# Query projection in four wide products instead of six, with the halves added on the vector engine

## The reference

```python
x = layer_norm(image_embeds, ln1_g, ln1_b)
l = layer_norm(latents, ln2_g, ln2_b)
q = l @ Wq
kv = jnp.concatenate([x, l], axis=1) @ Wkv
k, v = jnp.split(kv, 2, axis=-1)
w = jax.nn.softmax(einsum('bhqd,bhkd->bhqk', q * scale, k * scale))
out = einsum('bhqk,bhkd->bhqd', w, v)        # then out @ Wo, the residual, the experts
```

## Time and profile before

| | |
|---|---|
| median of 3 runs | 1283.3 us (1283.28 to 1284.77) |
| the profiled execution's own time | 1282.83 us |
| its span, first to last instruction | 1281.1 us |
| mean granted PE clock | 0.989 of full speed |
| PE busy / DVE busy / ACT busy | 1229.3 / 880.0 / 762.5 us |

### The profile page before, as it was taken

The page is one execution under the profiler, slowest core; times in us unless marked ns, Lnnn a source line. Parts: engine busy times, 40 slices in busy tenths (PEclk is TensorE's granted clock), DMA queues, the critical chain, the costliest instruction groups (busy, mean ns, idle before and its releaser), DMA issues. The chain is left out here.

```text
span 1281.1 us, 28175 instructions
## 1 busy us (share of the span) xinstructions
PE 1229.3 (96%) x8954; PEld 1014.5 (79%) x8954; DVE 880.0 (69%) x2643; ACT 762.5 (60%) x2231; POOL 459.5 (36%) x638
## 2 busy tenths in 40 slices
PE   5999999999999999999999999999999999999995
PEld 4788888888887888788878887888888878787774
DVE  6766777777777777777767776777776666444564
ACT  5676666666666666666666665666666643344442
POOL 4222323333332333233323332333332322354564
PEclk9999999999999999999999999999999999999998
DMA  9900000000000000000000000000000173445576
GB/s 292 320 15 2 1 13 1 29 2 28 9 21 4 28 2 29 3 29 2 29 3 29 2 29 3 29 2 29 1 26 1 59 225 101 124 141 187 187 233 212
DMA packets 68495, 79.29 MB, mean 62 GB/s; under 512 B 7584, under 2 KB 60784, under 8 KB 68336
## 3 DMA queue, kind: packets, MB, share of 16 engines
q1 hardware_dynamic: 60472, 56.18, 14.7%
q0 software_dynamic: 6912, 18.95, 3.9%
q10 hardware_dynamic: 952, 2.18, 0.5%
HBM read 39.38 MB, written 37.90 MB: 60 GB/s over the span
## 5 line engine op out<-in xcount | busy, mean ns | idle before, releaser
L1161 ACT ACTIVATE probs<-st,neg_max 128x333 f32<-128x333 f32 x512 | 268.9, 538 | 269.3 <-DVE neg_max L1321 243.5
L1090 POOL TENSOR_TENSOR probs<-probs,inv_sum 128x333 f32<-128x333 f32 x128 | 94.8, 740 | 655.4 <-DVE inv_sum L1333 655.4
L1321 DVE TENSOR_REDUCE neg_max<-st 128x2 f32<-128x666 f32 x256 | 206.5, 845 | 128.2 <-PE st L1438 128.2
L1381 PE MATMUL ov<-PT,V 128*64 128x256 f32 (+1 forms) x1536 | 196.5, 391 | 0.1
L1422 PE MATMUL st<-ident,probs 128*128 128x128 f32 (+1 forms) x1536 | 189.0, 273 | 1.4 <-ACT probs L1161 1.4
L1422 PEld LDWEIGHTS st<-ident,probs 128*128 128x128 f32 (+1 forms) x1536 | 176.1, 143 | 5.0 <-issue 1.8
L1438 PE MATMUL st<-K_hl,Q_hl 64*128 64x334 f32 x1536 | 153.6, 332 | 14.6 <-issue 10.4
L1356 DVE COPY PT<-st 128x512 f32<-128x512 f32 x256 | 163.5, 680 | 0.0
L1392 PE MATMUL pj<-wkv,lT 128*128 128x512 f32 (+1 forms) x576 | 156.9, 407 | 3.3 <-DVE Q_hl L1337 1.6
L1381 PEld LDWEIGHTS ov<-PT,V 128*64 128x64 f32 (+1 forms) x1536 | 100.1, 138 | 64.4 <-issue 28.0
L1438 PEld LDWEIGHTS st<-K_hl,Q_hl 64*128 64x128 f32 x1536 | 118.7, 188 | 33.2 <-issue 18.4
(11 more groups left out here) (180 smaller groups left out, 1767.1 us busy)
## 6 DMA issues: line engine op xcount, KB each, us to landing
slots_x<-zeros SPq DMA_DIRECT2D x10, 1032.0 KB, 13.0
V<-slots_x SPq DMA_DIRECT2D x80, 129.0 KB
yg<-routed_y SPq DMA_DIRECT2D x32, 256.0 KB
h_kept<-h_turned SPq DMA_DIRECT2D x16, 256.0 KB, 2.5
hT<-h_kept SPq DMA_DIRECT2D x16, 256.0 KB, 3.3
out<-X SPq DMA_DIRECT2D x32, 128.0 KB
X<-in_x SPq DMA_DIRECT2D x2, 1024.0 KB, 13.6
w_gu<-in_L_ffn_expert_gate_w SPq DMA_DIRECT2D x2, 960.0 KB, 7.8
```

Of the source, the lines that this page charges most:

```text
L1090: pool.tensor_tensor(probs[:, v, 0, 0:SKV], probs[:, v, 0, 0:SKV], inv_sum[:, v, 0:1].to_broadcast([P, SKV]), ALU.mult).then_inc(normed, 1)
L1161: nc.scalar.activation(probs[:, v, i, 0:SKV], st_bank(i)[:, 0:SKV], ACT.Exp, bias=neg_max[:, v, i:i + 1], accum_out=sums[:, v, i:i + 1]).t ...
L1321: nc.vector.tensor_reduce(neg_max[:, v, 2 * i:2 * i + 2], st[i][:, :, 0:SKV], AX.X, ALU.max, negate=True).then_inc(maxed, 1)
L1381: last = nc.tensor.matmul(ov[half * HALF:(half + 1) * HALF, 0:SQ], V[0:kn, kt, head * DH:(head + 1) * DH], PT[0:kn, v, kt, half * SQ:(half ...
```

## The change

The six products of Q become four. The high weights of half k multiply the high and the low rows of half k in one product of 512 columns, which fills both halves of the bank: high rows in columns 0 to 255, low rows in columns 256 to 511. The low weights multiply the high rows into the second half (256 columns each). ACT takes the high part from the first half as before. DVE now needs two operations: what is left of the first half, into a new SBUF tile `Q_rest`, and then the second half plus `Q_rest`. The second waits for the first by a new semaphore `q_rest`, and it is the second that frees the bank.

```diff
+    Q_rest = sb("Q_rest", [P, SQ])
...
+    q_rest = sem("q_rest")
...
                 dve.wait_ge(q_hi, PAIRS * bb + u + 1)
-                nc.vector.scalar_tensor_tensor(Q_hl[:, r, 1, :], bank[:, 0:SQ], SCALE,
+                nc.vector.scalar_tensor_tensor(Q_rest[:], bank[:, 0:SQ], SCALE,
                                                Q_hl[:, r, 0, :].bitcast(F32), ALU.mult, ALU.subtract
-                                               ).then_inc(free, 1)
+                                               ).then_inc(q_rest, 1)
+                dve.wait_ge(q_rest, PAIRS * bb + u + 1)
+                nc.vector.scalar_tensor_tensor(Q_hl[:, r, 1, :], bank[:, SQ:2 * SQ], SCALE, Q_rest[:],
+                                               ALU.mult, ALU.add).then_inc(free, 1)
...
-                split3(bank[:, 0:SQ], lambda a, k: wq[:, a, k, p * P:(p + 1) * P],
-                       lambda a, k: lT[:, w, a, k, 0:SQ]).then_inc(pj_full, 1)
+                both = bank[:].rearrange("p (a t) -> p a t", a=2)
+                mm(both, wq[:, 0, 0, p * P:(p + 1) * P], lT[:, w, :, 0, 0:SQ], start=True, stop=False)
+                for k in range(KD):
+                    mm(bank[:, SQ:2 * SQ], wq[:, 1, k, p * P:(p + 1) * P], lT[:, w, 0, k, 0:SQ],
+                       start=False, stop=False)
+                last = mm(both, wq[:, 0, 1, p * P:(p + 1) * P], lT[:, w, :, 1, 0:SQ], start=False, stop=True)
+                last.then_inc(pj_full, 1)
```

## The result

The changed kernel takes 1300.15 us (median; runs of 1296.84, 1297.24, 1303.07 and 1305.47), the kernel before 1283.44 (1283.28 to 1284.77): the medians differ by 16.7 us, and the ratio on record, which is taken over the runs and not from the two medians, is 1.0141 (95% interval 1.0118 to 1.0164). Forecast were 1296 us (+12.8), range 1289 to 1302. The direction, the mechanism and the range held; the sum came out 4 us small. The two faster runs have a mean granted clock of 0.988 and 0.990, the two slower ones 0.984 and 0.980; the clock turns out to be one of the terms that I had made too small. The profiled execution is the one of 1303.07 us; its span is 1301.3, 20.2 above that of before.

The account below looks back on a forecast made before the run. PE, busy 96%, was taken to bound the kernel; 14.1 us of stops where PE waits for DVE's added 0.46 us, less 1.3 us of PE time, gave +12.8 us, so 1296 us, range 1289 to 1302.

Parts of the forecast that it names:

- PE's blocks: Q's products on PE: four take nearly the time of six, 0.01 us off a pair, 1.3 us off in all.
- p = 2, V: Batch's pair 2: V's load waits for Q's bank, cover 0.07 us, stop 0.40 us in ten batches; 4.6 us in all.
- p = 6, V: Batch's pair 6: V's load waits for Q's bank, cover 0.26 us, stop 0.21 us ten times; 2.1 us.
- p = 7, scores: Batch's pair 7: next scores wait for DVE's copies, no cover; 0.32 us in 12 steps, loop turns left out; 3.8 us.
- p = 3, router: Batch's pair 3: router's product waits for the output's low part; 0.20 us eight times, other steps added; 2.5 us together.
- p = 0: Batch's pair 0: cover 0.53 us, so no stop except 0.1 us each in two steps at the loop's turns.
- start: Steps 0 and 1: V already waits for DVE, so each pays 0.46 us; 0.9 us.
- rival (c): PE's products: instructions count, not columns; 0.24 us a pair saved, 30 us, giving 1277 us; chance 0.04.
- rival (a): DVE's two operations on Q: the wait costs nothing, spacing 0.34 us, sum +6.8, 1290 us; chance 0.10.
- Rival (b): V's load and DVE: the added operation is hidden in all but the start; 1283 us; chance 0.06.
- rival (d): DVE's two-source operation from PSUM holds longer, 0.57 us, and cover in p = 0 goes too; +19 us, 1302 us; chance 0.14.
- rival (e): Half-clock stretches behind the loop's turns: none or all four turns show one, -3.6 or +1.2 us, 1292 to 1297; chance 0.10.

Follow-up runs that it names:

- e2: Against the changed kernel: four products kept, but one DVE operation, the bank's second half left out of Q; 1282.14 us, ratio 0.999.
- e3: Against the changed kernel: the second DVE operation reads Q's high part instead of the first one's result and waits for nothing; 1292.05 us, ratio 1.0074.
- e4: Against the changed kernel: the output's low part stands between the two DVE operations on Q; 1300.1 us, ratio 1.0128.
- e1: Against the changed kernel: six products as before, but still two dependent DVE operations; 1304.14 us, ratio 1.0163.
- e5: Against the kernel before: wide products and two DVE operations only in pairs p = 1, 4 and 5 of each batch; 1288.68 us, ratio 1.0036.
- u_after: Against the changed kernel: the loop written out in full, every step in its place; 1280.1 us, ratio 0.9976.

## Why the prediction came out as it did

Forecast and measured by place (us, profiled executions). The measured sum of a place is that of the interval in which its stop lies; PE's blocks are what remains to the 18.6 us by which the last scores start later (1043.1 us against 1024.4). "Found" is the range over the steps of a place:

| place | forecast | measured | single stop: forecast, found |
|---|---|---|---|
| PE's blocks | -1.3 | -2.0 | 0.01, 0.02 a step |
| p = 2, V | 4.6 | 4.4 | 0.40, 0.40 |
| p = 6, V | 2.1 | 3.6 | 0.21; 0.19 or 0.52 |
| p = 7, scores | 3.8 | 5.7 | 0.32, 0.31; at the turns 0, 0.49 to 0.73 |
| p = 3, router | 2.5 | 1.5 | 0.20; 0.15 to 0.19 |
| p = 1, V | 0 | 0.8 | 0; 0.15 in five steps |
| p = 0 | 0.2 | 4.0 | behind three turns 1.1 to 1.6 |
| start | 0.9 | 0.6 | |
| sum | 12.8 | 18.6 | |

This is the execution of 1303 us. Two of the four runs lie at +13.4 and +13.8.

- **Bottleneck and PE's side: right.** Four products take the time of six; rival (c) wanted 0.24 us off a block of 0.82, and a gain of 30 us in e2, which shows 1.3 us and an interval (0.9977 to 1.0003) that can't be told from no gain. The prediction held a section of the Trainium skill against the trace there ("TensorE: Matmul & The Clock Gate", Part 3, The mechanism). That section also names a second case in which a load is pulled ahead, the background weight buffer, and with this case the hidden loads of 0.19 us agree.
- **DVE's step: right.** 0.46 us, seen at 482.91 and 483.37; e3 takes 0.12 of it out by taking the dependency out, and the time falls by 8 us. That is rival (a)'s difference (I had priced it at 6), and it decides against (a). What the Trainium skill says of it ("VectorE: DVE Perf Modes", The DRAIN you can't avoid), that the semaphore between two such operations costs nothing extra, isn't borne out here: 0.46 us with the wait, 0.34 without (e3). The prediction left out that the same section says itself that a next operation which isn't held starts earlier; the 0.34 us agree with that sentence. Rival (b) falls by 26 waits of V's load where there were 2, rival (d) by a spacing of 0.46 and not 0.57.
- **Cover and stop at p = 2, 7 and 3: right** to 0.03 us outside the turns, each time by the same subtraction: spacing less cover. It also foretold which way e4 would move each of them.
- **p = 6: the term was mis-sized**, 2.1 us for a measured 3.6. The cover was read rightly: V's load comes 0.30 to 0.33 us behind Q's low part in all ten steps of the kernel before. In five steps the stop is 0.19 us, as forecast. In the other five it is 0.52, because there DVE stops 0.29 us for its own instructions ahead of Q's operations. That stop is new: neither the kernel before nor e2 has it, while after, e1, e3 and e4 all have it in the same five steps, and no kernel with its loop written out has one over 0.15 us. So no reading of more steps in the trace of before would have found it. What places it there isn't shown.
- **p = 7 at the turns: a term put at nothing that measured 2.4 us.** I left out four steps, since the turn "stops PE for over 2 us anyway". By place these four are 0.49 to 0.73 us longer each. Here PE before and after at one turn:

```profile
521.27 1.19 PE L1438 MATMUL st<-K_hl,Q_hl 64*128 64x334 f32 x12 [2.56 <-issue]
```

```profile
528.75 0.55 PE L1443 MATMUL st<-K_hl,Q_hl 64*128 64x334 f32 x3 [3.28 <-issue]
```

  It is tempting to say that what arrives late at the turn leaves later, but the other traces don't bear it out. In all, the four stops are 10.4 us before and 12.7 after; they are 11.6 us in e2, which has one operation, and in e4, which has two, they are those of before:

```profile
PE st L1445 <- issue: 10.4, 4, 2.7
```

  So about half of the growth also comes without the added operation, and with it there can be none. What sets the length of this stop stays open; each of the kernels with a loop has one trace, and how much the stop varies from run to run isn't known.
- **The clock behind the turns: rival (e)'s sign, its size too small.** Rival (e) had -3.6 to +1.2 us. Part of that was a reading: the window of the earlier trace rows begins after the stretch does. The 3.5 us before it, behind the same turn in the kernel before, are already at 0.84:

```profile
391.00:394.50 3.50, 2.64 (x22) 1.90 (x24) 1.87 (x4) 0.99 (x4) 0.00 (x0) 0.84 0.03 9
```

  So this stretch cost 3.5 x 0.16 + 3.5 x 0.33 = 1.7 us and not 1.2. Windows behind the second and the third turn of after; the column behind POOL is the granted clock:

```profile
530.00:533.50 3.50, 3.50 (x16) 2.03 (x17) 3.42 (x15) 2.19 (x8) 0.00 (x0) 0.52 0.00 0
...
659.00:663.50 4.50, 2.89 (x18) 2.19 (x20) 1.66 (x3) 0.77 (x3) 0.00 (x0) 0.60 0.02 7
663.50:667.00 3.50, 3.50 (x16) 2.21 (x13) 2.35 (x14) 1.48 (x7) 0.98 (x2) 0.54 0.00 0
```

  After, two of the turns show a stretch twice as long as those of before, and one that had none has one. Behind these three turns p = 0 is 1.1 to 1.6 us longer, 4.0 us in sum. That this belongs to the change isn't shown: in e2, with one operation, all four turns have a stretch, and p = 0 behind them is 1.8 us longer than before. The two faster runs have the higher mean clock, 0.988 and 0.990 against 0.984 and 0.980; 0.005 of 1300 us is 6.5 us, about what parts 1297 us from 1303 to 1305. Only the mean is on record for them, so where in the run the difference lies isn't known. Multiplying each run's time by its clock takes the clock out, as an estimate, and then the change costs 14 to 15 us over the kernel before, in the median.

The errors are thus, in the order of the table: -0.7, -0.2, +1.5, +1.9, -1.0, +0.8, +3.8 and -0.3, together +5.8 on the profiled execution. Three steps carry it, p = 6, the turns at p = 7 and the clock behind them, and none of the three could be read in full from the trace of before; and for the median of the runs, in which the clock is better, 4 us remain.

The -1.0 at p = 3 is for the most part no effect of the change. The first two such steps lost 0.27 and 0.40 us, as forecast, and eight others 0.15 to 0.19. But of the three where the router's product waits behind a DMA, two came out 0.31 and 0.46 us shorter than before, where I had added 0.07 each. In e2, which loses nothing at DVE, the same two steps are 0.57 and 0.54 us shorter. The sum is thus lower by a gain that the forecast did not have.

## What to carry to other kernels

Trading instructions of the busiest engine for one of an engine that is 69% busy is not decided by the shares but by cover: list each place where the busiest engine takes something from the other, subtract how far ahead it comes, and multiply what is left. That subtraction was right to 0.03 us at three kinds of places (p = 2, 3 and 7). Keep a margin for what it can't see: an added instruction came with a stop of 0.3 us of DVE's own instruction supply in a place where the old trace had none, and the stops at the loop's turns and the clock behind them came out several us apart between kernels with the same waits. Matmul columns, not instructions, were what PE paid for, so putting two narrow products side by side bought 0.02 us where 0.46 was given for it.

## What the runs showed of the chip

- A dependent vector operation (128x256, 4 bytes) costs 0.12 us more than an independent one: spacings of 0.46 and 0.34 us behind an operation of 0.42.
- Writing out the loop makes the kernel 11 us faster (1272.13), and the four stops at its turns alone were 10.4. With the cover that DVE gains (0.23 to 0.27 us instead of 0.07 to 0.13 at p = 2) the change then costs 8 us instead of 17.
- The four stops at the turns are 10.4 us (before, e4), 11.1 (e5), 11.6 (e2), 12.0 (e1) and 12.7 (after). They don't follow the number of operations on DVE.
- DVE, too, stops for its instructions, 0.29 us in five of the ten steps p = 6 of the changed kernel, none of them in the kernel before.
- A stretch at half clock needs no turn of the loop. In u_after one stands at 490 us; the last stop of PE before it is one of 0.79 us at 488.45, for the output's low part. The window:

```profile
490.00:493.50 3.50, 3.50 (x25) 2.25 (x25) 1.71 (x4) 1.60 (x7) 1.57 (x2) 0.64 0.21 76
```

What starts such a stretch, and how long it lasts, stays open: no run here moved the clock without moving PE's stops.
